# A four-layer metaformer on one core: the combination of routed experts, the token norm of the attention and its q, k, v products in one block of eight groups

## The reference, cut to what matters

```python
t = t + _L0_ffn_ref(_ln_t(t), ...)      # each token: gate1 * y[expert1] + gate2 * y[expert2]
x = _from_tokens(t, x)
x = x + _L1_conv_ref(_ln_c(x), ...)     # attention in each image, 8 heads of 8
...
def qkv(W0, b0, W1, b1):
    t = jnp.concatenate([x0 + _lin(x0, W0, b0), x1 + _lin(x1, W1, b1)], axis=-1)
qn = q / jnp.maximum(jnp.linalg.norm(q, axis=-1, keepdims=True), eps)
kn = k / jnp.maximum(jnp.linalg.norm(k, axis=-1, keepdims=True), eps)
attn = einsum(qn, kn) * scale + bias; softmax; @ v; projection
```

## Time and profile before

| | us |
|---|---|
| median of three runs | 1069.72 |
| lowest and highest | 1069.62, 1072.52 |
| the profiled execution: its own time | 1068.35 |
| its span, first to last instruction | 1066.6 |
| busy in the span: PE, DVE, ACT, POOL | 854.2, 705.6, 629.0, 302.8 |
| mean granted clock of TensorE, share of full speed | 0.888 |

### The profile page before, as it was taken

How to read it: one execution, slowest core, us unless ns; L and a number is a source line. 1 busy time by engine, 2 the same in 40 slices (tenths; PEclk the granted TensorE clock), 3 DMA queues, 4 the chain that set the end, 5 groups by cost and what they waited for, 6 DMA issues and landing times. The chain is left out here.

```text
span 1066.6 us, 21175 instructions
## 1 busy us (share of the span) xinstructions
PE 854.2 (80%) x6842; PEld 575.1 (54%) x6842; DVE 705.6 (66%) x1796; ACT 629.0 (59%) x1289; POOL 302.8 (28%) x337
## 2 busy tenths in 40 slices
PE   4993379999999346688888949995859999958497
PEld 2772249999999235466666634443533444425232
DVE  7796776644444369688888866886774545446775
ACT  4652135544444436788888736885746777746353
POOL 3155137777777343200000020111230101025100
PEclk9896599999999665699999968997987999979699
DMA  4001733300100201011111000002000000000000
GB/s 133 2 1 38 103 85 94 89 21 21 25 25 17 86 14 40 11 61 39 59 39 46 25 20 2 1 1 62 1 0 2 0 0 0 1 22 1 2 1 39
DMA packets 25272, 32.71 MB, mean 31 GB/s; under 512 B 11582, under 2 KB 14665, under 8 KB 24814
## 3 DMA queue, kind: packets, MB, share of 16 engines
q1 hardware_dynamic: 20206, 27.50, 9.1%
q0 software_dynamic: 4992, 4.22, 1.6%
HBM read 19.31 MB, written 4.91 MB: 23 GB/s over the span
## 5 line engine op out<-in xcount | busy, mean ns | idle before, releaser
L1829 DVE SCALAR_TENSOR_TENSOR routed_hid_stage<-ps,routed_act_stage 128x512 f32<-128x512 f32 (+1 forms) x117 | 70.4, 603 | 98.7 <-ACT routed_act_stage L1602 97.3
L1602 ACT ACTIVATE routed_act_stage<-ps 128x512 f32<-128x512 f32 x117 | 69.9, 597 | 87.3 <-PE ps L1914 87.2
L1924 PE MATMUL ps<-w_sb,routed_hid_stage 128*128 x936 | 117.4, 269 | 0.0
L1152 ACT ACTIVATE hid_stage<-ps,b_col_sb 128x512 f32<-128x512 f32 x192 | 116.1, 695 | 0.4 <-PE ps L1103 0.3
L1914 PE MATMUL ps<-routed_x_stage,w_sb 128*128 128x256 f16 x858 | 114.5, 275 | 1.8 <-ACT routed_x_stage L1610 1.0
L1924 PEld LDWEIGHTS ps<-w_sb,routed_hid_stage 128*128 128x128 f32 x936 | 113.6, 192 | 1.4
L412 POOL TENSOR_TENSOR st_sb<-st_sb,neg_half_sb 128x4 f32 (+1 forms) x32 | 37.5, 1172 | 251.7 <-DVE st_sb L407 251.7
L1658 POOL DMA_INDIRECT routed_got_stage<-expert_rows,take_stage x78 | 82.5, 1058 | 61.6 <-DVE give_stage L1800 38.1
L1103 PE MATMUL ps<-x_sb,w_sb 128*128 (+1 forms) x384 | 97.9, 401 | 1.8 <-ACT hid_stage L1152 1.8
L1117 PE MATMUL ps<-hid_stage,w_sb 128*64 128x512 f32 x384 | 94.4, 610 | 1.3 <-DVE gated_stage L1184 1.3
L1914 PEld LDWEIGHTS ps<-routed_x_stage,w_sb 128*128 x858 | 84.0, 103 | 10.2 <-issue 2.3
(11 more groups left out here) (395 smaller groups left out, 1833.3 us busy)
## 6 DMA issues: line engine op xcount, KB each, us to landing
w_stage_sb<-f_w SPq DMA_DIRECT2D x32, 176.0 KB
x_sb<-w_sb SPq DMA_DIRECT2D x16, 256.0 KB, 2.4
rt_sb<-vals_stage SPq DMA_DIRECT2D x16, 256.0 KB, 2.3
rel_bias_sb<-bias_bands SPq DMA_DIRECT2D x16, 128.0 KB
w_stage_sb<-f_w SPq DMA_DIRECT2D x14, 128.0 KB, 3.0
w_sb<-f_w SPq DMA_DIRECT2D x1, 1536.0 KB
routed_got_stage<-expert_rows,take_stage POOLq DMA_INDIRECT x78, 2.5
expert_out<-routed_rows_stage,give_stage POOLq DMA_INDIRECT x78, 2.2
```

The costliest lines, as they stand in the source:

```text
L1152: nc.scalar.activation(hid[:, n % RING, :], ps[:, n % BATCH, :], func, bias=b1_col[:, b:b + 1], scale=UNSCALE).then_inc(h_act, 1)
L1602: nc.scalar.activation(act_h[:, n, :], ps[:, H1 + (q + n) % 2, :], ACT.Silu, scale=UNSCALE).then_inc(h_act, 1)
L1829: last = nc.vector.scalar_tensor_tensor(hid[:, q % 2, n, 0:full], ps[:, H3 + (q + n) % 2, 0:full], UNSCALE, act_h[:, n, 0:full], ALU.mult, ...
L1924: last = nc.tensor.matmul(ps[:, Y + q % 2, h * C:(h + 1) * C], hid[:, q % 2, n, a * BLK + h * P:a * BLK + (h + 1) * P], w2[:, bass.ds(e * ...
```

## The change

The three stretches 1 to 3 become one block after the experts' stream. The experts' block ends with SP's loads: 16 DMAs of four tiles each, four for every pair of groups (a quarter, with a semaphore `y_landed` of its own), and nothing in that block waits for them. The second rows of groups 4 to 7 go to a free part of `w16`, since `sq` is shared with the squares of q and k.

In the new block each engine works in steps s, on several groups of different stages:

- **SP**: the loads of `qkv_w`, `proj_w`, `scale` and the small weights, now at the start of this block.
- **DVE** first waits for these loads and prepares `scale` and `qkv_w`; then in step s: the norm's sum of squares and variance of group s-1; after `summed` of group s, the norm's sum and centring; the heads' sum of squares of s-3 (`floor_pair` if s is even); the weighting of the first rows of s+1; the norm's scaling of s-1; `split_parts` of s-5; `invert` of pair (s-3)//2 if s is even. Steps run from -1 to 12.
- **ACT**: the Exp of `scale`, the padding of `vals` (one instruction, 128 x 5888); then in step s: weighting of the second rows of s+1 (four instructions), square of s, copy of s-1 to `xn_ch`, `take_products` of s-2, `root` if s is even, `take_turned` of s-6.
- **POOL**: the power of s-1, the two additions to `x_tok` of s+1, the doubling of s-5.
- **PE**: `product` of s-2, `turn` of s-6, the norm's transposes of s-1 into bank 6 or 7. `turn` now has one pair of banks, 4 and 5, so that group g waits until ACT has copied group g-1.

Some loads of the first stage are counted on `loaded["f"]` in place of two other semaphores, and in `convolution` two semaphores become one with two counts.

```diff
-                    for h, s in enumerate(halves):
-                        for k, dst in enumerate((xn_tok, sq)):
-                            sp.dma_start(dst[:, s, :], slots_d...[k, :, s, :]).then_inc(y_loaded[h], 16)
+                    for n in range(QUARTERS):
+                        for g in (2 * n, 2 * n + 1):
+                            for k, dst in enumerate((xn_tok[:, group_tiles(g), :], second_rows(g))):
+                                sp.dma_start(dst, by_slot[k, :, group_tiles(g), :]).then_inc(y_landed[n], 16)
...
-            norm_stage(1e-6, beside=Beside())
...
             # PE
                     def turn(g):
                         pe.wait_ge(split, g + 1)
-                        if g >= 2:
-                            pe.wait_ge(t_copied, g - 1)
+                        if g >= 1:
+                            pe.wait_ge(t_copied, g)
...
+                    pe.wait_ge(setup, IDENTITY_ADDED)
+                    for s in range(GROUPS + 6):
+                        if 0 <= s - 2 < GROUPS:
+                            product(s - 2)
+                        if 0 <= s - 6 < GROUPS:
+                            turn(s - 6)
+                        if 0 <= s - 1 < GROUPS:
+                            token_norm.turn(pe, s - 1)
             # ACT
+                    act.wait_ge(setup, SCALED)
+                    nc.scalar.activation(scale_h, scale_h, ACT.Exp).then_inc(rooted, 1)
+                    nc.scalar.activation(vals[:, :, :, VW:], idn[:, 0:1]...broadcast_to(...), ACT.Copy, scale=0.0)
+                    for s in range(-1, GROUPS + 6):
+                        if s + 1 < GROUPS:
+                            weight_second(s + 1)
+                        if 0 <= s < GROUPS:
+                            token_norm.square(act, s)
+                        if 0 <= s - 1 < GROUPS:
+                            token_norm.copy(act, s - 1)
+                        if 0 <= s - 2 < GROUPS:
+                            take_products(s - 2)
+                        if s >= 4 and s % 2 == 0 and s - 3 < GROUPS:
+                            root((s - 3) // 2)
+                        if 0 <= s - 6 < GROUPS:
+                            take_turned(s - 6)
             # POOL
+                    def combine(g):
+                        xg, second = x_tok[:, group_tiles(g), :], second_rows(g)
+                        pool.wait_ge(y_gated, g + 1)
+                        c.link(nc.gpsimd.tensor_tensor(xg, xg, xn_tok[:, group_tiles(g), :], ALU.add))
+                        pool.wait_ge(y_gated_act, g + 1)
+                        nc.gpsimd.tensor_tensor(xg, xg, second, ALU.add).then_inc(summed, 1)
...
+                    for s in range(-1, GROUPS + 5):
+                        if 0 <= s - 1 < GROUPS:
+                            token_norm.power(pool, s - 1)
+                        if s + 1 < GROUPS:
+                            combine(s + 1)
+                        if 0 <= s - 5 < GROUPS:
+                            double(s - 5)
             # DVE
+                    dve.wait_ge(loaded["l1"], want["l1"])
...
+                    for s in range(-1, GROUPS + 5):
+                        if 0 <= s - 1 < GROUPS:
+                            token_norm.sum_squares(dve, s - 1)
+                            token_norm.variance(dve, s - 1)
+                        if 0 <= s < GROUPS:
+                            dve.wait_ge(summed, s + 1)
+                            token_norm.sum(dve, s)
+                            token_norm.centre(dve, s)
+                        if 0 <= s - 3 < GROUPS:
+                            sum_squares(s - 3)
+                            if s % 2 == 0:
+                                floor_pair((s - 3) // 2)
+                        if s + 1 < GROUPS:
+                            weight(s + 1)
+                        if 0 <= s - 1 < GROUPS:
+                            token_norm.scale(dve, s - 1)
+                        if 0 <= s - 5 < GROUPS:
+                            split_parts(s - 5)
+                        if s >= 4 and s % 2 == 0 and s - 3 < GROUPS:
+                            invert((s - 3) // 2)
```

More of the change, by code:

```diff
@@ L234, in _ @@
                         prepare_experts(prepare, sp=sp)
-                if beside is not None:
-                    @block.sync
-                    def _(sp):
-                        beside.sync(sp)
                 @block.vector
@@ L259, in _ @@
                         prepare_experts(prepare, dve=dve)
-                    if beside is not None:
-                        beside.vector(dve)
                     for h, s in enumerate(halves):
@@ L297, in _ @@
                         prepare_experts(prepare, act=act)
-                    if beside is not None:
-                        beside.scalar(act)
                     if stacked:
@@ L326, in _ @@
                         nc.gpsimd.memset(gate_parts[:, :, :], 0.0)
-                    if beside is not None:
-                        beside.gpsimd(pool)
                 @block.tensor
@@ L504, in low, with __init__, square, sum_squares @@
                                                x16[0:C, self.columns(g)], ALU.mult, ALU.subtract).then_inc(g_copied, 1)
+        class GroupNormPlain(GroupNormInPlace):
+            def __init__(self, eps, banks, squares):
+                GroupNorm.__init__(self, eps, False, banks[0])
+                self.banks, self.squares = banks, squares
+                self.prior = [max((h for h in range(g) if banks[h] == banks[g]), default=None) for g in range(GROUPS)]
+            def square(self, act, g):
+                act.wait_ge(g_centred, g + (self.n0 + 1))
+                nc.scalar.activation(self.squares(g), xn_tok[:, self.tiles(g), :],
+                                     ACT.Square).then_inc(g_squared, 1)
+            def sum_squares(self, dve, g):
+                dve.wait_ge(g_squared, g + (self.n0 + 1))
+                nc.vector.tensor_reduce(st[:, 1, self.tiles(g)], self.squares(g), AX.X,
+                                        ALU.add).then_inc(g_link, 2)
+            def copy(self, act, g):
+                act.wait_ge(g_turned, g + (self.n0 + 1))
+                nc.scalar.copy(xn_ch[0:C, self.columns(g)], self.turned(g)).then_inc(g_copied, 1)
         def linear_attention():
@@ L1631, in _ @@
                     stream(step)
-                    for h, s in enumerate(halves):
-                        act.wait_ge(y_loaded[h], 32)
-                        for t in range(s.start, s.stop):
-                            last = nc.scalar.activation(sq[:, t, :], sq[:, t, :], ACT.Copy, scale=gates[:, 1, t:t + 1])
-                        last.then_inc(rows_by_act, 1)
                 @block.gpsimd
@@ L2047, in _ @@
                 def _(sp):
+                    load(sp, "l1", qkv_w[:, :], L1["qkv_w"])
+                    load(sp, "l1", proj_w[:, :], L1["proj_w"])
+                    load(sp, "l1", scale[:, :], L1["scale"].unsqueeze(0).broadcast_to((P, 2 * HEADS1)))
+                    load_small(sp, F1)
                     sp.wait_ge(t_copied, 1)
@@ L2107, in take_turned, with weight_second @@
                         for b in range(2):
-                            last = nc.scalar.copy(qk_t[:, 2 * g + b, :], ps[:, 4 + 2 * (g % 2) + b, :].bitcast(F16))
+                            last = nc.scalar.copy(qk_t[:, 2 * g + b, :], ps[:, TURNED + b, :].bitcast(F16))
                         last.then_inc(t_copied, 1)
-                    for g in range(GROUPS + 6):
-                        if g < GROUPS:
-                            take_products(g)
-                        if g >= 2 and g % 2 == 0 and g <= GROUPS:
-                            root(g // 2 - 1)
-                        if g >= 6:
-                            take_turned(g - 6)
+                    def weight_second(g):
+                        second = second_rows(g)
+                        wait_landed(act, g)
+                        for t in range(TPG):
+                            last = nc.scalar.activation(second[:, t, :], second[:, t, :], ACT.Copy,
+                                                        scale=top_gates[:, 1, g * TPG + t:g * TPG + t + 1])
+                        last.then_inc(y_gated_act, 1)
@@ L2171, in split_parts @@
                         last.then_inc(halved, 1)
-                    for g in range(GROUPS + 3):
-                        if g < GROUPS:
-                            sum_squares(g)
-                            if g % 2:
-                                floor_pair(g // 2)
-                        if g >= 2 and g % 2 == 0 and g <= GROUPS:
-                            invert(g // 2 - 1)
-                        if g >= 3:
-                            split_parts(g - 3)
+                    for s in range(-1, GROUPS + 5):
[18 more added lines that the diff above has]
+                            invert((s - 3) // 2)
             s_ps, shifted, exped = sem("l1_s_ps"), sem("l1_shifted"), sem("l1_exped")
```

126 lines of the change are left out of this document (64 added, 62 removed).

## The result

| | before | after |
|---|---|---|
| median of 4 runs each, us | 1069.67 | 1082.43 |
| lowest and highest | 1068.57, 1072.52 | 1081.35, 1084.06 |
| the profiled execution: its own time, its span | 1068.35, 1066.6 | 1082.37, 1080.6 |
| mean granted clock | 0.888 | 0.882 |
| first load of expert rows to ACT's last copy into `qk_t` | 78.95 | 94.29 |

The changed kernel is slower: ratio 1.0124, interval [1.0093, 1.0156]. Four more runs of it on another chip, beside 17 of before, gave 1.0101 [1.0066, 1.0136]. Within the changed stretch 15.3 us were lost; over the whole span 14.0, on the medians 12.8.

A forecast was written before the change was run, and what follows sets the result against it. Bounds: DVE's work and the longest loop through engines in fixed order. A walk of priced instructions ended at 456.0; plus 1.1 shortfall, minus 2.6 for clock, gave 454.5, 15.8 later; on the median 1069.7, about 1085.5, range 1074 to 1090.

The forecast's parts named there:

- The start: Merged block's beginning: loads, preparation and 5.0 us padding put DVE's first sum at 378.3; before, the norm began at 375.2.
- The filling: First steps of the merged block: chained waits through PE and ACT put invert of pair 0 at 402.3.
- The steady part: Middle of the block: a two-step loop through engines takes 15.7 per pair, against DVE's own work of 13.1.
- The drain: Block's end: with one pair of banks, turn and ACT's copy alternate, 3.92 per group for four groups, ending at 456.0.
- the -2.6 for the clock: Taken off the predicted stretch end, for PE's clock being a third of the way to its upper level.
- The upper clock: Rival: PE keeps its upper clock in the merged block, halving its share of each loop: +9.8, 1079.5; chance 0.2.
- The work as the bound: Rival: in the merged block DVE runs through without waiting for ACT, 9.3 earlier, 1060.4; chance 0.07.
- Contention: POOL's additions and doublings beside DVE's scaling and splitting, slowed by shared SBUF interfaces: end 1 to 2 us later.
- (a): Block's start: order costs time because everything stands behind layer 1's loads and ACT's padding; late preparation expected to save 7.9.
- (b): ACT's root stands behind the norm's copy and take_products; moving it ahead was expected to save 6.0 us.
- (c): Only one pair of banks for turn; a second pair was expected to save 3.0 us at the end.
- (d): PE's lower clock lengthens the root's wait on ACT; spares everywhere were expected to save 7 to 9 us of stretch.

The follow-up runs named there:

- The late start: Changed kernel with scale and qkv_w prepared a step later and the padding in eight pieces on POOL: stretch 88.31, 1074.03 us.
- The single edits: Runs of the changed kernel with one experiment's edit each, such as root placement, banks or spare PE products: from 1074.03 to 1084.06 us.
- the run with the root early: Changed kernel with ACT's root ahead of the norm's copy and take_products: stretch 88.57, 1080.76 us.
- three edits: Changed kernel with root ahead of the norm's copy, two pairs of banks for turn, and late preparation with padding in pieces on POOL: 1068.72 us.
- the shortest version: Changed kernel with root, banks, late preparation, PE/ACT reordering, later invert, and spare PE products in the filling: stretch 74.62, 1066.26 us.
- PE's and ACT's order: On top of root, banks and late preparation: ACT takes products before the norm's copy, PE transposes the norm before turn: stretch 78.41, 1067.58 us.
- the six edits: Changed kernel with root, banks, late preparation, ACT and PE reordered, and invert a step later, without spare products: stretch 77.43, 1066.38 us.

## Why the prediction was right

Predicted 1085.5 in a range of 1074 to 1090, slower with 0.88; measured 1082.43. By its steps:

- **The start.** Loads over near 367.3: 366.91 + 0.43 = 367.34. DVE's first instruction 371.0: 371.29. Padding 5.0: 5.09. First sum 378.3: 378.56. The late start confirms that the start was exposed (6.0 us of stretch); how it divides between the padding and the wait for the loads is only estimated above.
- **The filling.** `invert` of pair 0 at 402.3: 401.27, a wait of 4.71 in front of it. Right within 1 us. The single edits show what lies in it: the root's place on ACT is worth 3.3, the clock 2.8.
- **The steady part.** Two pairs of 15.7: 15.04 and 14.81. The loop is there as described; in the second pair its steps can be followed in the rows above, and each of them is 0.1 to 0.3 shorter than my price, because within one engine the profile shows an instruction starting before the record of the one ahead ends. But "over 2 us each time" in front of `invert` was wrong for the second one: 0.89. DVE's own work for the first pair was not 13.1 but 14.07 with its small gaps (the run with the root early), so that DVE's work was nearly as long as the loop.
- **The drain.** 3.92 for a group: 448.27 to 452.25 is 3.98. End at 454.5: 452.25 + 1.93 = 454.18. That this is so near is in part luck: the walk's 456.0 was 1.8 too late; the +1.1 for its shortfall and the -2.6 for the clock are not shown, and the granted clock was below what I assumed (0.50 from 390 to 420, with PE busy 8.59 of 10 in the first ten and 8.70 in the last; the only spell at the upper level was between 429 and 433). The -2.6 is no third of the way either: 456.0 less 447.4 is 8.6, of which a third is 2.9. The mis-sized terms are the pairs, -1.6 together, `invert` 0, -1.0, and the drain from `invert` 2 on, 23.1 in place of 22.4.
- **"Nothing behind the stretch depends on more than its end"** was the step that failed: 1.7 us came back between the two table loads around layer 1's experts, where the clock rose sooner, and 1.5 by the end. The 3 us between 1085.5 and 1082.4 are 0.3 of the end of the stretch, these 1.5, and 1.2 by which the medians lie nearer together than the two profiled spans.
- **The rivals.** The upper clock did not hold. The work as the bound (1060.4) is refuted for the changed kernel, and its condition was in part right: with the loops opened DVE stands at 9.4 of 10 for a while, but no version came under 74.6. DVE was busy 53.2 us with three edits and 52.7 in the shortest version, some 3 more than in the changed kernel, beside the pieces of padding on POOL; the rest of the stretch lies mostly in the filling and the drain. That DVE is the bound of these versions is argued from its busy time and not shown by an edit.
- **Contention** was put at 1 to 2 us. The durations show it (below). The end moved by 0.7 when the additions went to DVE, a balance with the 6.7 us that DVE took on, so its price by itself stays open.

The theory stands for (a), (b) and (c), each by its own edit, and together they give 14.6 us where the single ones sum to 13.7. For (d) only the filling is shown. Whether the 1.3 us of PE's and ACT's order are the norm's transposes or the copy was not separated.

## What to carry to other kernels

Before merging blocks into one pipeline, write down for each step the longest loop through all engines, not only the work of the busiest: an instruction that others wait for (here a root of 0.31 us) belongs on its engine ahead of the long copies that nobody waits for yet. A merged block has one start: what its first instruction waits for, and what stands on each engine ahead of the first group's work, is paid in full, where separate blocks had hidden it. Work moved to an engine that looks idle is not free when it slows a neighbour: the padding on POOL held DVE. And if the work of the bounding engine does not shrink, the merging can bring at most that engine's idle time, here 27.0 us of 78.95 before; the six edits won 1.5 of it, a quarter of a per cent of the whole time.

## What the runs showed of the hardware

- **DVE and POOL.** In the changed kernel at 406.45, beside POOL's two additions, DVE's first product of `split_parts` took 1.21 us and the conversion behind it 0.84, where alone they take 0.69 and 0.43; POOL's additions took 0.84 and 1.06 in place of 0.72. With the additions on DVE the mean of that product fell from 0.842 to 0.709. POOL's first addition ran until 407.12; 407.12 + 0.69 = 407.81, and DVE was over at 407.66. The same holds at 412.04, where DVE's scaling, 0.42 alone, took 0.99 and ended at 413.03, beside an addition that ran until 412.75. The numbers look like taking turns, less some 0.15 us, and not like sharing. The Trainium skill (SBUF — State Buffer, SBUF: two separate sides) calls the pair of ports an exclusive lock for a whole instruction; these rows agree to 0.15 us.
- **DVE beside a fill on POOL.** With the padding as one fill of 5.01 us on POOL, DVE's minimum over 128 x 8 elements took 2.53 us in place of 0.17 and ended 0.02 behind the fill; in pieces of 0.71 us the variance over 128 x 4 took 0.90. Before, DVE's scaling over 128 x 1024 started at 387.72, took 1.23, and ran beside the same fill (388.03, 5.06 us), where alone it took 1.25. So the fill holds some of DVE's instructions and not others.
- **The clock.** It was granted at 0.50 from 390 to 400 with PE busy 8.59 of 10 us in the changed kernel, and at 0.94 in the same stretch with 8.07 before: PE's busy share in a stretch does not say which level it gets. Ahead of the rise, at about 391, PE had worked without a gap since 386.14 in before; in the changed kernel it stood idle in each step.
- **Identical code differs.** Layer 1's experts and what follows, up to the next table load, took from 152.41 to 159.93 us in the profiled executions. In the two compared above the clock rose at different places; whether that explains all of it was not tried. That is more than most of the effects here, and it is why a stretch repeats to 0.2 us and a median to 2.
- **The table load.** 1.28 us, and the root starts 0.02 behind its end in the changed kernel too (399.63 + 1.28, 400.93).
